# Two tile sizes for the expert pass of a routed vision block, and an earlier first tile

## The reference

```python
h = tok(x)                                  # (64, 196, 192): 64 images, 196 patches each
h = h + attn(layernorm(h))                  # 12 heads, a 3x3 neighbour sum taken off the scores
h = h + ffn(layernorm(h))
def ffn(x):                                 # E = 8 experts, K = 2, D = 192, F = 768
    score = relu(x @ Wr1.T + br1) @ Wr2.T + br2
    w = softmax over the two largest scores, 0 elsewhere
    out = 0
    for e in range(8):
        out += w[..., e:e+1] * (relu(x @ W1[e].T + b1[e]) @ W2[e].T + b2[e])
```

## Time and profile before

| | |
|---|---|
| median of 3 runs | 2048.9 us |
| span of the profiled execution | 2041.0 us |
| first hidden matmul of an expert tile | 1206.69 us |
| last group routed, iteration 49 begins | 1797.01 us |
| PE busy in the span | 1849.8 us (91%) |
| POOL busy in the span | 1139.5 us (56%) |

### The profile page before, as it was taken

The page is one execution under the profiler, slowest core; times in us unless marked ns, Lnnn a source line. Parts: engine busy times, 40 slices in busy tenths (PEclk is TensorE's granted clock), DMA queues, the critical chain, the costliest instruction groups (busy, mean ns, idle before and its releaser), DMA issues. The chain is left out here.

```text
span 2041.0 us, 54475 instructions
## 1 busy us (share of the span) xinstructions
PE 1849.8 (91%) x18013; PEld 1378.2 (68%) x18013; DVE 1458.3 (71%) x4506; ACT 1287.1 (63%) x2661; POOL 1139.5 (56%) x1070
## 2 busy tenths in 40 slices
PE   4898998899889989898898579999999999999996
PEld 4666766666666666666665457777777777767774
DVE  4798889888988898889887456565665655574442
ACT  4688888888888888888888334444444444433332
POOL 4345464645555555555552356766767667664444
PEclk8898999999999999999998569999999999999998
DMA  4586665656566565656554358887888889878985
GB/s 154 147 253 195 186 203 166 196 181 192 174 191 189 179 185 180 194 185 192 174 173 120 102 175 194 197 211 192 199 216 195 198 206 197 198 188 182 187 183 83
DMA packets 362520, 373.10 MB, mean 183 GB/s; under 512 B 144516, under 2 KB 326080, under 8 KB 358272
## 3 DMA queue, kind: packets, MB, share of 16 engines
q1 hardware_dynamic: 320704, 329.03, 55.3%
q0 software_dynamic: 41664, 42.12, 12.3%
HBM read 223.20 MB, written 125.83 MB: 171 GB/s over the span
## 5 line engine op out<-in xcount | busy, mean ns | idle before, releaser
L2021 ACT ACTIVATE mh<-mid_bank 128x512 bf16<-128x512 f32 x336 | 200.6, 597 | 415.2 <-PE mid_bank L1622 415.2
L1923 DVE SCALAR_TENSOR_TENSOR ml<-mid_bank,mh 128x512 bf16<-128x512 f32 x336 | 232.0, 690 | 320.0 <-ACT mh L2021 319.3
L874 DVE TENSOR_REDUCE row_max<-s_bank 98x2 f32<-98x392 f32 x768 | 394.2, 554 | 53.6 <-PE s_bank L650 51.6
L1072 ACT ACTIVATE probs<-t_bank 98x392 f32<-98x392 f32 x768 | 339.7, 499 | 103.9 <-PE t_bank L666 100.5
L2097 POOL DMA_INDIRECT out_rows<-y_out,tail x168 | 267.4, 1592 | 160.7 <-DVE y_out L1957 114.1
L1636 PE MATMUL y_bank<-wst,mh 128*128 128x192 bf16 x1344 | 330.7, 246 | 0.8 <-DVE y_out L1957 0.8
L1639 PE MATMUL y_bank<-wst,ml 128*128 128x192 bf16 x1344 | 330.7, 246 | 0.0
L1638 PE MATMUL y_bank<-wst,mh 128*128 128x192 bf16 x1344 | 330.5, 246 | 0.0
L650 PE MATMUL s_bank<-k_stack,q_stack 96*98 96x196 f16 x1536 | 234.6, 259 | 46.2 <-DVE row_max L874 32.9
L1248 POOL TENSOR_TENSOR x_lo<-x_buf,x_hi 128x588 f16<-128x588 f32 x128 | 170.5, 1344 | 175.1 <-DVE x_b L939 73.0
L666 PE MATMUL t_bank<-q_stack,k_stack 104*98 104x196 f16 x1536 | 225.3, 259 | 32.8 <-ACT probs L1072 29.6
(11 more groups left out here) (257 smaller groups left out, 4527.6 us busy)
## 6 DMA issues: line engine op xcount, KB each, us to landing
wst<-packed SPq DMA_DIRECT2D x56, 1584.0 KB, 8.3
x_buf<-in_x_t SPq DMA_DIRECT2D x32, 1176.0 KB, 7.9
q_stack<-stack_parts SPq DMA_DIRECT2D x288, 98.0 KB, 2.5
k_stack<-stack_parts SPq DMA_DIRECT2D x288, 98.0 KB, 2.6
stack_parts<-qk_hi SPq DMA_DIRECT2D x32, 588.0 KB, 2.9
stack_parts<-qk_lo SPq DMA_DIRECT2D x32, 588.0 KB, 3.1
out_rows<-h_buf SPq DMA_DIRECT2D x32, 294.0 KB
h_in<-out_rows SPq DMA_DIRECT2D x32, 294.0 KB
```

Of the source, the lines that this page charges most:

```text
L874: nc.vector.reduce_max(row_max[st.odd][:, :, hh:hh + 1], s_bank[hh % 2][0:HALF, :, 0:TOKENS], AX.X).then_inc(max_ready, 1)
L1072: nc.scalar.activation(probs[st.odd][:, hh], t_bank[hh % 2][0:HALF, :, 0:TOKENS], ACT.Exp).then_inc(probs_ready, 1)
L1923: nc.vector.scalar_tensor_tensor(ml[n % MID][:], mid_bank[n % MID_PS][:], 0.0, mh[n % MID][:], ALU.max, ALU.subtract).then_inc(ml_ready, 1)
L2021: nc.scalar.activation(mh[n % MID][:], mid_bank[n % MID_PS][:], ACT.Relu).then_inc(mh_ready, 1)
```

## The change

Tiles have 512 rows (`BIG`) or 256 (`LITTLE`). A planner at build time goes through the groups and takes, after each, a tile of 512 if that many rows are certain for some expert, else one of 256, which needs 8 x 255 + 1 = 2041 listed rows: four groups. After the last group it takes tiles of 256 while these are certain, and the rest in 256s. This gives 8 tiles of 256 (after groups 4 to 11), 38 of 512 (12 to 49), 7 of 256 that are certain and 14 of 256 for the rest: 67 tiles.

A step is still 512 columns wide: for a little tile it holds two chunks of 128 hidden units with 256 rows each, so a little tile has three steps. While groups are routed, an iteration computes one tile: a little one has its steps at c = 0, 2, 4. After the last group steps follow each other without gaps, two little tiles to an iteration. `evicted` becomes two semaphores, one for each `y_bank`; a little tile uses one bank, evicted by ScalarE if its number is even and by VectorE if it is odd. The waits are counted in steps and rows of tiles of either size. In an iteration POOL sends at c = 2, and adds where the step order puts them. The eight choices after the last group stand at eight successive steps, from iteration 49, c = 3, on. The rest is planned from iteration 51 instead of 50.

```diff
-T = 512
-TJ = T // P
-NT = (2 * ROWS_ALL + EXPERTS * (T - 1)) // T
-FULL = (2 * ROWS_ALL - EXPERTS * (T - 1) + T - 1) // T
+BIG = 512
+LITTLE = 256
+BANK = 512
+SHIFT = 8
+TJ = LITTLE // P
...
-SELECT = EXPERTS
-COMPUTE = SELECT + 2
-REST = NT - FULL
...
+def certain(size):
+    return EXPERTS * (size - 1) + 1
+def plan_tiles():
+    sizes, groups, rows = [], [], 0
+    for g in range(1, FGROUPS + 1):
+        rows += 2 * GT
+        for size in (BIG, LITTLE):
+            if rows >= certain(size):
+                sizes.append(size)
+                groups.append(g)
+                rows -= size
+                break
+    while rows >= certain(LITTLE):
+        sizes.append(LITTLE)
+        groups.append(FGROUPS)
+        rows -= LITTLE
+    full = len(sizes)
+    rest = (rows + EXPERTS * (LITTLE - 1)) // LITTLE
+    return sizes + rest * [LITTLE], groups, full, rest
+SIZES, GROUPS_FOR, FULL, REST = plan_tiles()
+NT = len(SIZES)
+COMPUTE = GROUPS_FOR[0] + 2
+STEP_LIST = [(i, c) for i in range(NT) for c in range(0, FCH, BANK // SIZES[i])]
+NSTEPS = len(STEP_LIST)
+ENDS = list(itertools.accumulate(FCH * SIZES[i] // BANK for i in range(NT)))
+ROWS_TO = list(itertools.accumulate(SIZES[i] // P for i in range(NT)))
+def place_steps():
+    at, n, it = {}, 0, COMPUTE
+    while n < NSTEPS + LAG:
+        alone = n < NSTEPS and SIZES[STEP_LIST[n][0]] == LITTLE and STEP_LIST[n][0] < FULL
+        alone = alone and GROUPS_FOR[STEP_LIST[n][0]] < FGROUPS
+        for c in range(0, FCH, 2 if alone else 1):
+            at[it, c] = n
+            n += 1
+        it += 1
+    return at, it
+STEP_AT, ITERATIONS = place_steps()
...
+        def y_place(i, j):
+            return (j // 2 if SIZES[i] == BIG else i % 2), j % 2
...
-                    for g in range(SELECT - 1):
+                    for g in range(GROUPS_FOR[0]):
                         sp.wait_ge(sent[g], SENT)
-                last = i + SELECT - 1
-                if last < FGROUPS:
-                    sp.wait_ge(sent[last % RING], SENT * (last // RING + 1))
-                sp.dma_start_transpose(xT[q][:].bitcast(U16), slots[bass.ds(at, T), 0:XROW]).then_inc(xT_in[q], 16)
+                elif i < FULL and GROUPS_FOR[i] > GROUPS_FOR[i - 1]:
+                    g = GROUPS_FOR[i] - 1
+                    sp.wait_ge(sent[g % RING], SENT * (g // RING + 1))
+                sp.dma_start_transpose(rows_of(i).bitcast(U16), slots[bass.ds(at, size), 0:XROW]
+                                       ).then_inc(xT_in[q], 16)
                 wait(sp, gate_step, gate_steps(i - DEEP + 1))
-                wait(sp, added, 16 * TJ * (i - DEEP + 1))
-                sp.dma_start(tail[q][:], slots[bass.ds(at, T), XROW:XROW + TAIL].rearrange("(j p) c -> p j c", p=P)
-                             ).then_inc(tail_in[q], 16)
+                wait(sp, added, 16 * rows_to(i - DEEP))
+                sp.dma_start(tail[q][:, 0:size // P], slots[bass.ds(at, size), XROW:XROW + TAIL]
+                             .rearrange("(j p) c -> p j c", p=P)).then_inc(tail_in[q], 16)
 
             for g in range(AHEAD):
                 load_rows(g)
-            for it in range(ITERATIONS):
+            for it in range(FGROUPS):
                 load_rows(it + AHEAD)
-                if tile_there(it - SELECT):
-                    load_tile(it - SELECT)
-            sp.wait_ge(added, 16 * TJ * NT)
+                if it in GROUPS_FOR:
+                    load_tile(GROUPS_FOR.index(it))
+            for i in range(GROUPS_FOR.index(FGROUPS), NT):
+                load_tile(i)
...
+                for k in range(BANK // size):
+                    c = c0 + k
+                    o = mid_bank[n % MID_PS][:, k * size:(k + 1) * size]
+                    def w(b, rows=P):
+                        at = b * PART + (c % PCHUNKS) * P
+                        return wst[q][0:rows, c // PCHUNKS, at:at + P].bitcast(F16)
...
+                if c0 == 0:
+                    for bank in range(2):
+                        if parts_in(i, bank):
+                            wait(pe, evicted[bank], evictions_to(i - 1, bank))
...
+                    n = STEP_AT.get((it, c))
+                    if n is not None and n < NSTEPS:
+                        take_low_mid(n)
+                    if n is not None and n - LAG + 1 in ENDS:
+                        evict(ENDS.index(n - LAG + 1))
                     if c == 0:
                         gates(it - 1)
                     elif c == 2:
                         find_place(it - 1)
                     elif c == 3:
+                    late = FCH * (it - FGROUPS) + c - 3
+                    if late >= 0:
+                        select(GROUPS_FOR.index(FGROUPS) + late)
+                    elif c == 3 and it in GROUPS_FOR:
+                        select(GROUPS_FOR.index(it))
+                    if n is not None and n < NSTEPS:
+                        i = STEP_LIST[n][0]
+                        if n == steps_to(i) - (2 if SIZES[i] == BIG else 1):
+                            tile_gates(i)
...
-                    wait(pool, added, 16 * TJ * i)
-                    for j in range(TJ):
+                    wait(pool, added, 16 * rows_to(i - 1))
+                    for j in range(SIZES[i] // P):
...
-            for it in range(ITERATIONS + 1):
+            for it in range(ITERATIONS):
                 number_tokens(it)
-                add_rows(it - COMPUTE - 1)
-                send(it - 1)
+                for c in range(FCH):
+                    if c == 2:
+                        send(it - 1)
+                    n = STEP_AT.get((it, c))
+                    if n is not None and n - LAG + 1 in ENDS:
+                        add_rows(ENDS.index(n - LAG + 1))
```

More of the change, by code:

```diff
@@ L1475, in expert_phase @@
         used = sem("used")
-        evicted = sem("evicted")
+        evicted = [sem(f"evicted{i}") for i in range(2)]
         added = sem("added")
@@ L1502, in tile_there, with steps_to, rows_to, y_at @@
             return 0 <= i < NT
+        def steps_to(i):
+            return ENDS[i] if i >= 0 else 0
+        def rows_to(i):
+            return ROWS_TO[i] if i >= 0 else 0
+        def y_place(i, j):
+            return (j // 2 if SIZES[i] == BIG else i % 2), j % 2
+        def y_at(i, j):
+            bank, half = y_place(i, j)
+            return y_bank[bank][:, half, 0:DIM]
+        def parts_in(i, bank):
+            return [j for j in range(SIZES[i] // P) if y_place(i, j)[0] == bank]
+        def evictions_to(i, bank):
+            return sum(len(parts_in(k, bank)) for k in range(i + 1))
+        def rows_of(i):
+            q = i % DEEP
+            return xT[q][:, 0:3 * SIZES[i]].rearrange("p (b t) -> p b t", b=3)
         block = ctx.enter_context(nc.Block())
@@ L1624, in project @@
+                last.then_inc(mid_ready, 1)
             def project(n):
-                i, c = n // FCH, n % FCH
-                q = i % DEEP
+                i, c0 = STEP_LIST[n]
+                q, size = i % DEEP, SIZES[i]
                 pe.wait_ge(ml_ready, n + 1)
[L1628 to L1632, removed]
@@ new lines, in project @@
+                for k in range(BANK // size):
+                    c = c0 + k
+                    at = W1_COLS + (c % PCHUNKS) * DIM
+                    high = wst[q][:, c // PCHUNKS, at:at + DIM]
+                    low = wst[q][:, c // PCHUNKS, W2_COLS + at:W2_COLS + at + DIM]
+                    for j in range(size // P):
+                        cols = slice(k * size + j * P, k * size + (j + 1) * P)
+                        o = y_at(i, j)
+                        nc.tensor.matmul(o, mh[n % MID][:, cols], high, start=(c == 0 and j % 2 == 0), stop=False,
+                                         skip_group_check=True)
+                        nc.tensor.matmul(o, mh[n % MID][:, cols], low, start=False, stop=False, skip_group_check=True)
+                        last = nc.tensor.matmul(o, ml[n % MID][:, cols], high, start=False, stop=False,
+                                                skip_group_check=True)
@@ L1641, in project @@
                 if c == FCH - 1:
[L1642 to L1645, removed]
+                    for j in range(size // P):
+                        last = nc.tensor.matmul(y_at(i, j), three[:], wst[q][:, :, PACK - BIAS_COLS:], start=False,
+                                                stop=True, skip_group_check=True)
@@ L1668, in _ @@
                         router_scores(it)
[L1669 to L1670 removed]
+                    list_others(FCH * (it - REST_AT) + c - LAG)
+                    if n is not None and 0 <= n - LAG < NSTEPS:
                         project(n - LAG)
@@ L2039, in _ @@
             copy_edge(0)
-            for it in range(COMPUTE, ITERATIONS + 1):
-                i = it - COMPUTE
+            for it in range(COMPUTE, ITERATIONS):
                 for c in range(FCH):
-                    if tile_there(i):
-                        take_high_mid(FCH * i + c)
```

(3 more changed lines are left out.)

159 lines of the change are left out of this document (76 added, 83 removed).

## The result

The changed kernel takes 2092.1 us (median of 4 runs, 2085.6 to 2095.8); the kernel before, beside it on the same chip, 2051.1. The ratio is 1.0204, interval 1.0181 to 1.0227: 2.0% slower, where the prediction said 1.5% (2079, range 2025 to 2106).

What follows compares the result with a forecast made beforehand. The prediction took TensorE to bound most of the expert phase, nearly tied with serial adds at the end. Start -20.6, light iterations +27, end +24 made 2079 us, 30 slower (1.5%); range 2025 to 2106.

Steps and rivals of the forecast that it cites:

- First tile after four groups: Start of the expert phase: four sends fewer at 5.14 us bring the first expert matmul 20.6 us earlier.
- Eight light iterations at 11.0 us: Little tiles during routing: 21.6 us from routing to rows over two iterations; 88 us in all, net +27.
- 35 full iterations at 15.14, matmuls of 256 columns at nothing: Middle, routing with 512-row tiles: 530 us, unchanged per iteration; narrower matmuls cost nothing, 9 us at most.
- The little tiles at the end at 10.0 us: After routing: serial chain of 0.3 link, 1.86 add period and landing about 8; 18 tiles take 180 us.
- the row taken as nearest: Add at 1808.33 beside weights issued at 1809.09: landed about 8.0 us after the weights' issue, 8.8 after its own.
- if D shrinks, the cycle stops near 8.3: End: if the last add's landing time D falls, loads waiting for landings still hold the cycle near 8.3 us.
- early landings: Rival, end: fewer queued adds land sooner beside weights loads, cycle 8.3, 31 us less, 2048; chance 0.18.
- TensorE did not stay the bound: Concerns the rival for the end that adds are hidden and TensorE's 6.39 us a tile binds: 2008; chance 0.14.
- The clock did fall: Concerns the rival that idle TensorE drops to 1.2 GHz at the end, 12.8 us a tile: +50, 2129; chance 0.05.
- Light iterations don't get lighter: Rival, little tiles during routing: iterations stay at 15.14 us each, +33, 2112; chance 0.05.
- The last stretch: From iteration 49 to POOL's last add: predicted 24 us longer, with more tiles added serially.
- The 7.9 us around the span: Difference of profiled span 2041.0 and median 2048.9, taken to lie around the span and carried over unchanged.

Runs made afterwards that it cites:

- runs 7 and 8: Changed kernel (7), and its version with little tiles only while few groups are routed (8), given four buffers and a three-iteration lead: 2068.9 and 2054.5 us.
- run 3: Changed kernel with odd tiles' adds sent to a second table, so adds wait only for those of the tile two before: 2060.2 us, ratio 1.0029.
- run 5: Changed kernel with six instead of three buffers for the small table of tokens and weights: 2055.0 us beside 2048.9, ratio 1.0030.
- run 4: Changed kernel loading only half of the weights (792 of 1584 KB) from the second tile after the last group on: 2056.3 us, ratio 1.0015.

## Why the prediction was right, and where its steps were off

*First tile after four groups*: -20.6 predicted, -19.4 measured.

*Eight light iterations at 11.0 us*: the mechanism was right (rows needed two iterations after their routing; runs 7 and 8), the size was 11.9, 7 us more in all. My 21.6 us for the latency took the landings from medians of the whole kernel and the way to the sends from an estimate; a pair of iterations takes 24.4, of which no run separates the parts.

*35 full iterations at 15.14, matmuls of 256 columns at nothing*: the 15.13 us are there unchanged; nothing contradicts the rest.

*The little tiles at the end at 10.0 us*: 10.01 measured, and taking the serial wait away (run 3) gives 34 us back. The parts of the 10.0 were off in both directions by the same half microsecond, and that the total hit is luck: the landing is 7.4 on average instead of 7.8, and from a landing to POOL's next add it is 0.78 instead of 0.3. The 0.78 stood in the rows: 1947.12 + 7.54 = 1954.66 and the next add at 1955.43. Leaving it out also lengthened the nearest landing: the add of 1808.33 was taken to land when POOL began again at 1817.16, 8.8 us after its issue; less 0.78, it is 8.0.

*What a landing is made of*: the row taken as nearest was the right one. What the prediction saw but used only for the time of the weights load was that SP's small load waits for a landing. It argued "if D shrinks, the cycle stops near 8.3" from that wait as if it were a side limit, and the expectation of run 5 treated it as harmless. Run 5 shows that it fixes the bad phase of every load: 7.9 us without it. So the 10.0 us are a loop of two links, the serial adds and the loads that wait for them: taking away either gives back nearly the same (34 us in run 3, 35 in run 5). The rule of the Trainium skill ("Trainium Kernel Development and Optimization", Key Constraints) that queues share the 16 engines and interleave had been weighed as speaking for early landings; the landings of 3.6 and 8.0 us in run 5 show a load delaying an add, which agrees with sharing, and halving the queued adds alone did not make them early.

*The rivals.* TensorE did not stay the bound. The clock did fall, for short times: 0.90 of full speed was granted over the end's window, where that rival had 0.5 throughout. In the 17 cycles from 1896.74 on it cost nothing, since every pair of adds began 0.78 us after a landing and none waited for TensorE; what it cost in the light iterations (0.87) no run separates. "Light iterations don't get lighter" was right by a fifth: they took 11.9, between 11.0 and 15.1.

*The last stretch* was 3 to 4 us cheaper than predicted: adds of the last tiles of 512 had fallen behind less. The first pair of a little tile after them began 58.9 us after iteration 49 (1885.40), where the sum has 65.8; the rest of the stretch took 3 to 4 us more than summed.

*The 7.9 us around the span* were a wrong reading. In every run 1.7 to 1.9 us lie around the span; the other 6 were that the profiled execution before was shorter than the median. As the sum carries the term over unchanged, the forecast difference of 30 us does not depend on it.

*A reading without effect*: the send at 1198.96 is the first of the ninth group. So it gives the 5.14 us a group rightly, but the last send that the first tile needs is the one before it, 3.9 and not 2.6 us before the transposed load:

```profile
1197.66 0.96 POOL L2082 DMA_INDIRECT slots<-row_r,spot  x1 [0.30 <-issue]
```

## What to carry to other kernels

Halving a tile halves only what scales with its rows. Write down per tile what does not (weights load, one landing in a serial chain, one wait), and the tile can't take less than the longest chain of them. And look at what a prefetch's issue waits for: a small load with a short buffer, in the same queue ahead of a large one, set the time of the large one; three more small tables turned +2.0% into +0.3%, and with a longer lead it became -1.2%.

## What the runs showed of the hardware

An indirect add of 128 rows lands 3.6 us after its issue starts when no weights load is issued near it, and 8.0 us when 1584 KB are issued 0.33 us after it (run 5). With 1584 KB issued some 0.65 us before it, it lands after 7.4 us on average (changed kernel); with 792 KB there, after 6.0 (run 4). When POOL waits for a landing, its next indirect add begins 0.77 to 0.78 us after it, in the kernel before as in the changed one. The DMA engines carried 243 GB/s over 160 us of small tiles at a busy share of 0.95 (run 5), against 183 GB/s at 0.87 in the same stage before. The attention phase of 1160 us, all but unchanged, varies by 15 us from one profiled execution to the next (1157.8 to 1173.1), so spans of two single executions are no measure of a change of this size; landmarks inside them are.
